# Mixing weights scaled and summed from an SBUF table, in place of fp32 kernel sums kept in DRAM: an adaptive mixing and FFN kernel on one Trainium2 core

## What is computed

```python
# cond: one 64x64 mixing matrix and a bias per sample
h = gelu(cond @ W0 + b0); h = gelu(h @ W1 + b1)
att = softmax(h @ W2 + b2)                         # [128 samples, K=8]
agg_w = einsum('bk,koi->boi', att, weight)         # [128, 64, 64]
agg_b = att @ bias_k
y = einsum('boi,bih->boh', agg_w, x) + agg_b[:, :, None]
# ffn on the rows of y (D = 1024)
base = einsum('bsd,od->bso', y, base_W)
logits = einsum('bsd,ed->bse', y, router_W)        # E = 8 experts, top 2
mid = einsum('bsd,edr->bser', y, lora_A) * gate    # R = 16
out = x + base + 2 * einsum('bser,erd->bsd', mid, lora_B)
```

## Time and profile before

| | |
|---|---|
| median of 3 runs | 992.72 us (991.69 to 1067.75) |
| the profiled execution | 992.38 us |
| its span | 990.6 us |
| mean granted TensorE clock | 0.989 |
| TensorE busy | 963.9 us, 97% |
| VectorE busy | 686.5 us, 69% |
| ScalarE busy | 208.7 us, 21% |
| GpSimd busy | 330.5 us, 33% |
| DMA | 115.00 MB, 64145 packets, 38392 of them under 512 B |

### The profile page before, as it was taken

How to read it: one execution, slowest core, us unless ns; L and a number is a source line. 1 busy time by engine, 2 the same in 40 slices (tenths; PEclk the granted TensorE clock), 3 DMA queues, 4 the chain that set the end, 5 groups by cost and what they waited for, 6 DMA issues and landing times.

```text
span 990.6 us, 17707 instructions
## 1 busy us (share of the span) xinstructions
PE 963.9 (97%) x5742; PEld 882.8 (89%) x5742; DVE 686.5 (69%) x1529; ACT 208.7 (21%) x422; POOL 330.5 (33%) x245
## 2 busy tenths in 40 slices
PE   6788999999999999999999999999999999999998
PEld 4577999999999999999999999999999999999996
DVE  2878676677676667767667776766776766677674
ACT  3432121122211211212121121211212112122120
POOL 4904333322333322333332233333223333223331
PEclk9889999999999999999999999999999999999999
DMA  8324333433423333332343333334333233433311
GB/s 281 100 122 136 103 106 115 135 108 111 128 93 114 120 132 111 112 113 93 114 135 117 116 122 101 105 114 135 109 111 133 90 115 117 134 109 112 120 48 54
DMA packets 64145, 115.00 MB, mean 116 GB/s; under 512 B 38392, under 2 KB 38520, under 8 KB 63480
## 3 DMA queue, kind: packets, MB, share of 16 engines
q1 hardware_dynamic: 63856, 114.76, 35.0%
q10 hardware_dynamic: 272, 0.03, 0.0%
HBM read 79.01 MB, written 35.68 MB: 116 GB/s over the span
## 4 chain that ended last, share of the span: by engine, by line
PE 91%; issue 4%; POOL 2%; DMA 1%; DVE 1%; SPq 0%; POOLq 0%; DVEq 0%
PE pc L504 17%; PE pa L515 13%; PE pb L515 13%; PE y_ps L476 11%; PE pb L518 9%; PE pa L518 9%; PE pd L504 9%; PE pc L536 4%; PE pd L536 4%; DMA c_raw<-in_base_t 1%; PE pd L526 1%; POOL w_raw L360 1%; POOL w_raw L348 1%; POOL lb_lo L395 0%; DVE out_sb L910 0%
## 5 line engine op out<-in xcount | busy, mean ns | idle before, releaser
L405 POOL TENSOR_TENSOR out_sb<-out_sb,u 128x512 f32<-128x512 f32 x96 | 136.4, 1451 | 209.1 <-DVE u L956 209.1
L476 PE MATMUL y_ps<-mix_w,x_sb 128*128 128x128 f32 x1024 | 199.5, 280 | 0.7 <-issue 0.7
L476 PEld LDWEIGHTS y_ps<-mix_w,x_sb 128*128 128x128 f32 x1024 | 171.9, 194 | 17.3 <-issue 3.9
L366 POOL TENSOR_TENSOR ya<-ya 128x512 f32<-128x512 f32 x32 | 42.6, 1331 | 420.7 <-DVE ya L850 420.7
L850 DVE TENSOR_TENSOR ya<-y_ps,bias_sb 128x512 f32<-128x512 f32 x128 | 87.7, 686 | 34.4 <-PE y_ps L476 31.3
L504 PE MATMUL pc<-w_hi,s_hi 128*128 128x512 f32 x256 | 106.8, 417 | 2.9 <-DVE out_sb L910 2.9
L515 PE MATMUL pa<-w_hi,a_hi 128*128 128x376 f32 x256 | 101.5, 397 | 6.2 <-DVE w_lo L802 6.2
L504 PE MATMUL pc<-w_hi,s_lo 128*128 128x512 f32 x256 | 101.2, 395 | 0.0
L504 PE MATMUL pc<-w_lo,s_hi 128*128 128x512 f32 x256 | 100.5, 393 | 0.0
L515 PE MATMUL pa<-w_lo,a_hi 128*128 128x376 f32 x256 | 86.3, 337 | 0.0
L515 PE MATMUL pa<-w_hi,a_lo 128*128 128x376 f32 x256 | 86.2, 337 | 0.0
(11 more groups left out here) (149 smaller groups left out, 2373.6 us busy)
## 6 DMA issues: line engine op xcount, KB each, us to landing
x_sb<-in_x SPq DMA_DIRECT2D x64, 512.0 KB, 3.4
out_sb<-in_x SPq DMA_DIRECT2D x64, 512.0 KB, 4.3
out<-out_sb SPq DMA_DIRECT2D x64, 512.0 KB, 2.8
bias_sb<-bias_rows SPq DMA_DIRECT2D x62, 64.0 KB, 5.2
agg_rows<-agg SPq DMA_DIRECT2D x1, 2048.0 KB, 9.1
mix_w<-agg_rows SPq DMA_DIRECT2D x120, 16.0 KB, 3.3
a_raw<-in_base_t SPq DMA_DIRECT2D x1, 1024.0 KB, 7.8
c_raw<-in_base_t SPq DMA_DIRECT2D x1, 1024.0 KB, 12.4
```

The source lines that it names most:

```text
L366: nc.gpsimd.tensor_tensor(y_block(0, 1), y_block(0, 1), y_block(0, 0), ALU.subtract).then_inc(s3_set, 1)
L405: nc.gpsimd.tensor_tensor(o, o, u2[:, :], ALU.add).then_inc(done, 1)
L476: mm = nc.tensor.matmul(y_ps[q % 2][:, j * P:(j + 1) * P], x_sb[m][:, c * P:(c + 1) * P], mix_w[m][:, :], start=True, stop=True)
```

## The change

The table mix_i (128 x 512: for each partition 64 outputs by 8 kernels, now laid out for both halves by the host and loaded in one DMA) stays in SBUF for the whole run. att_rows (128 x 512) holds for each partition its sample's eight attention values of all 64 tiles; it is made by one fp32 matmul from two small tables (parity, att_spread). For each tile n, m DVE multiplies the table with the tile's eight values (scale_mix) and sums over the kernels (sum_mix), and ACT copies the sum into the diagonal blocks (place_mix). The eight kernel sums, agg, agg_dram, mix_k and the DMAs of mix_w are gone. The scaled table of 128 x 512 lies over u2. b2 comes with params. The first loads stand in another order, and the warming transposes become fp32r matmuls of 512 columns. The core of the diff:

```diff
@@ sync
             sp.dma_start(mlp[:, :], params).then_inc(params_in, 16)
-            sp.dma_start(b2_sb[:, :], b2.partition_broadcast(P)).then_inc(b2_in, 16)
+            sp.dma_start(mix_i[:, :], mix_t).then_inc(mix_i_in, 16)
+            sp.dma_start(bk_sb[:, :], bias_k).then_inc(bk_in, 16)
             sp.dma_start(a_raw[:, :], base_t[0, :, :]).then_inc(a_in, 16)
-            for b in range(PAR):
-                sp.dma_start(mix_i[b * C:(b + 1) * C, :], mix_t).then_inc(mix_i_in, 16)
-            sp.dma_start(bk_sb[:, :], bias_k).then_inc(bk_in, 16)
-            for m in range(2):
-                sp.dma_start(x_sb[m][:, :], x_t[m, :, :]).then_inc(x_in[m], 16)
-            sp.dma_start(mix_k[:, :], mix_rows).then_inc(mix_k_in, 16)
+            sp.dma_start(x_sb[0][:, :], x_t[0, :, :]).then_inc(x_in[0], 16)
             sp.dma_start(w_raw[W_SIDE], side).then_inc(side_in, 16)
+            sp.dma_start(x_sb[1][:, :], x_t[1, :, :]).then_inc(x_in[1], 16)
...
                 next_x(n, m)
-                mixing_weights(2 * n + m, m, agg_dram)
                 mixing_bias(2 * n + m, m)
@@ tensor
-                    nc.tensor.transpose(pb[:, 0:P], ident[:, :], ident[:, :])
+                    nc.tensor.matmul(pb[:, 0:BANK], hot[:, 0:P], hot[:, :], start=True, stop=True)
...
-            pe.wait_ge(mix_k_in, 16)
-            mixing_kernels(0)
+            keep_warm(1)
             pe.wait_ge(bias_ready, 1)
...
             mm.then_inc(bias_bc_mm, 1)
+            keep_warm(2)
...
-                    if first(n):
-                        pe.wait_ge(mix_set[m], 2)
-                    else:
-                        pe.wait_ge(mix_w_in[m], MIX_W * n)
+                    pe.wait_ge(mix_set[m], PAR * n + PAR)
...
-                if q < 3:
-                    mixing_kernels(q + 1)
-            pe.wait_ge(agg_act, 2)
+                if q == 1:
+                    pe.wait_ge(spread_set, 1)
+                    nc.tensor.matmul(pb[:, BANK:], parity[:, :], att_spread[:, :], start=True,
+                                     stop=True).then_inc(att_rows_mm, 1)
@@ scalar
+            def place_mix(n, m):
+
+                act.wait_ge(summed_set, 2 * n + m + 1)
+                if first(n):
+                    act.wait_ge(zeros_set, 4)
+                else:
+                    act.wait_ge(mixed, 4 * n + m - 1)
                 for b in range(PAR):
...
@@ scalar, first_body
-                for n in range(4, NA):
-                    take_agg(n)
+                place_mix(1, 0)
                 for n in range(WP):
                     act.wait_ge(t1_made, n + 1)
                     take_hi(T1, n)
+                place_mix(1, 1)
                 act.wait_ge(lb_in, 16)
...
                 split_high(S3, 1, s3_set, 2)
+                place_mix(2, 0)
                 exponents(1)
                 split_high(A12, 1, y_ready, 8)
+                place_mix(2, 1)
@@ scalar, body
                     split_high(A12, p + 1, y_ready, 4 * p + 8)
+                mixes = not (isinstance(p, int) and p >= NP - 2)
+                if mixes:
+                    place_mix(p + 2, 0)
                 exponents(2 * p + 1)
+                if mixes:
+                    place_mix(p + 2, 1)
@@ vector
+            def scale_mix(n, m):
+
+                if first(n - 1 if isinstance(n, int) else n):
+                    dve.wait_ge(att_rows_set, 1)
+                dve.wait_ge(summed_set, 2 * n + m)
+                nc.vector.tensor_tensor(scaled[:, :].rearrange("p (c k) -> p c k", k=K),
+                                        mix_i[:, :].rearrange("p (c k) -> p c k", k=K),
+                                        att_rows[:, bass.ts(2 * n + m, K)].unsqueeze(1).broadcast_to(
+                                            [P, C, K]), ALU.mult).then_inc(scaled_set, 1)
+
+            def sum_mix(n, m):
+
+                dve.wait_ge(scaled_set, 2 * n + m + 1)
+                if not first(n):
+                    dve.wait_ge(mix_set[m], PAR * n)
+                nc.vector.tensor_reduce(summed[m][:, :], scaled[:, :].rearrange("p (c k) -> p c k", k=K), AX.X,
+                                        ALU.add).then_inc(summed_set, 1)
@@ vector, before the first body
             split_low(A12, 0)
+            scale_mix(1, 0)
+            sum_mix(1, 0)
             split_low(S3, 0)
@@ vector, first_body
                     take_lo(T3, n)
+                scale_mix(1, 1)
+                sum_mix(1, 1)
                 dve.wait_ge(t2_made, WP)
...
                 add_bias(1, 2)
+                dve.wait_ge(u2_in21, 1)
+                scale_mix(2, 0)
+                sum_mix(2, 0)
                 split_low(S3, 1)
...
                 split_low(A12, 1)
+                scale_mix(2, 1)
+                sum_mix(2, 1)
@@ vector, body
                 add_p5(p, k)
+                mixes = not (isinstance(p, int) and p >= NP - 2)
+                if mixes:
+                    dve.wait_ge(u2_in21, p + 1)
+                    scale_mix(p + 2, 0)
+                    sum_mix(p + 2, 0)
                 add_side_b(p)
                 add_up11_p74(p, k)
+                if mixes:
+                    scale_mix(p + 2, 1)
+                    sum_mix(p + 2, 1)
```

More of the change, by code:

```diff
@@ L3, with adaln_ffn_kernel @@
 from contextlib import ExitStack
-def adaln_ffn_kernel(nc, x, params, b2, mix_t, mix_rows, bias_k, base_t, side, lora_b, out):
+def adaln_ffn_kernel(nc, x, params, mix_t, bias_k, base_t, side, lora_b, out):
     f32, f32r = mybir.dt.float32, mybir.dt.float32r
@@ L112, in adaln_ffn_kernel @@
         _, warm = place("warm", 1)
+        _, mix_i = place("mix_i", C * K)
+        _, att_rows = place("att_rows", NT * K)
+        summed = [place(f"summed{m}", C)[1] for m in range(2)]
         assert top[0] <= 229344
@@ L132, in adaln_ffn_kernel @@
         b0_sb, b1_sb = (mlp[:, 3 * P + K + n:3 * P + K + n + 1] for n in range(2))
+        b2_sb = mlp[:, 3 * P + K + 2:3 * P + 2 * K + 2]
         h1, h2 = (over(f"h{n}", P, mlp_at + (3 + n) * P * 4 + 256) for n in range(2))
-        mix_i = over("mix_i", C * K, p1_at)
-        scaled = [over(f"scaled{m}", C * K, at) for m, at in enumerate((u2_at, s1_at))]
-        summed = [over(f"summed{m}", C, side_b_at + m * C * 4) for m in range(2)]
+        scaled = over("scaled", C * K, u2_at)
         pick_row = over("pick_row", 2 * PAR * P, ya_at)
         pick_half = over("pick_half", 2 * PAR * C, ya_at + 2 * PAR * P * 4)
+        hot = over("hot", BANK, ya_at + 2 * PAR * (P + C) * 4, f32r)
+        parity = over("parity", P, s2_at)
+        parity2 = over("parity2", PAR, s2_at + P * 4)
+        own_tile = over("own_tile", NT, s2_at + 2 * P * 4)
+        att_spread = over("att_spread", NT * K, s1_at)
         att_t = over("att_t", B, mid_at, parts=K)
@@ L141, in adaln_ffn_kernel @@
         bias_rows = over("bias_rows_sb", C, mid_at + 768)
-        att, b2_sb, att_n, att_nm, att_sum = (over(f"att{n}", c, mid_at + 1024 + n * 32) for n, c in enumerate(
-            (K, K, K, 1, 1)))
+        att, att_n, att_nm, att_sum = (over(f"att{n}", c, mid_at + 1024 + n * 32) for n, c in enumerate(
+            (K, K, 1, 1)))
         pa = ctx.enter_context(nc.psum_tensor("pa", [P, 2 * BANK], f32))
@@ L197, in adaln_ffn_kernel @@
         ROUTE = 12
-        NA = C * C // BANK
         def first(p):
@@ L256, in mixing_bias @@
                              bias_dram.rearrange("s (t r) -> t s r", t=NT)[t, :, :].partition_broadcast(P)
[L257 to L265, removed]
-                    else:
-                        src = agg_dram[r, :].rearrange("(i s c) -> i s c", i=C, s=2)
-                    sp.dma_start(dst[:, :, b, :], src).then_inc(mix_w_in[m], 16)
+                             ).then_inc(bias_in[m], 16)
             def next_x(n, m):
@@ L421, in keep_warm @@
                 for _ in range(times):
-                    nc.tensor.transpose(pb[:, 0:P], ident[:, :], ident[:, :])
[L424 to L433, removed]
+                    nc.tensor.matmul(pb[:, 0:BANK], hot[:, 0:P], hot[:, :], start=True, stop=True)
+            pe.wait_ge(hot_set, 1)
             pe.wait_ge(consts_set, 1)
-            keep_warm(3)
+            keep_warm(2)
             pe.wait_ge(params_in, 16)
@@ L692, in _ @@
                           bias_rows[:, :].rearrange("b (s c) -> b s c", s=2)).then_inc(bias_out, 16)
-            place_mix(0)
+            place_mix(0, 0)
             act.wait_ge(bias_bc_mm, 1)
@@ L698, in _ @@
                                ).then_inc(bias_set, 1)
-            take_agg(0)
-            place_mix(1)
-            take_agg(1)
+            place_mix(0, 1)
             act.wait_ge(side_in, 16)
```

78 lines of the change are left out of this document (35 added, 43 removed).

## The result

The changed kernel takes 1029.38 us (median of 4 runs, 1028.64 to 1030.52) against 993.0 (median of 4): a ratio of 1.0372, with a 95% interval of 1.0352 to 1.0392. One of the four runs of the kernel before took 1067.75 us, 7.6% above the other three, and is left out of the ratio. The forecast was 1036.4, in a range of 1015 to 1051, slower.

What follows compares the result with a forecast made beforehand. PE was taken to bound the kernel, busy 97% of the span and throughout the steady pairs. 992.4 + 29 x 1.6 for the pairs + 2.1 for the first body - 4.5 for the start = 1036.4 us, range 1015 to 1051.

Steps and rivals of the forecast that it cites:

- The pair: Steady loop: mid_lo comes late, so PE idles 1.6 us before up(0) in each of 29 pairs.
- the first place: After add_p5, before add_side_b: the first scaling waits for POOL, leaving the DVE queue 0.56 us late.
- the DRAM trip: Two copies of mixing weights from DRAM per tile, already hidden since PE never waits; removing them is worth 0.
- The address from a register: Scalings in the loop read att_rows at a register address; cost taken as 0, with 0.4 as the other end.
- The first pair: First body: same pieces, tighter, with POOL beside both scalings; loss of 2.1 us, bounds 1 and 3.
- rival C: PE idle time before up(0) lowers its clock to half speed in each pair: 1089 us, chance 0.04.
- The start: Before the steady pairs: earlier mixing brings B21's end forward; gain of 4.5 us, bounds 2 and 8.
- the parity product: New fp32 matmul with 512 columns in the start, taken to cost PE 2.0 us.
- the removed sums: Four of eight kernel sums gone before the first mixing, counted with the 3.53 us mix_k wait as 11.5 us.
- A: Delay stays hidden because DVE's idle 8.7 us a pair swallow the new 2.8: 987.9 us, chance 0.12.
- B: Queue order delays but no turns at the DVE/POOL port: 1.0 us a pair, 1019 us, chance 0.22.
- D: Much better start, all five waits and the eight sums' share gone, delay hidden: 970 us, chance 0.02.

Runs made afterwards that it cites:

- e1: Changed kernel with only ACT's copies of the second tile's sum moved behind mid_hi and keep_p1 of the next body: 1005.13 us, ratio 1.0125.
- e3: Changed kernel with only the second tile's scaling and sum moved into DVE's gap ahead of the even tile's routing: 986.87 us, ratio 0.9938.
- e4: Changed kernel with only the first tile's scaling and sum moved into DVE's gap ahead of the even tile's routing: 1021.61 us, ratio 1.0292.
- e2: Changed kernel with both tiles' scalings and sums moved into DVE's gap ahead of the even tile's routing: 985.88 us, ratio 0.9933.
- b1: Kernel before the change, with four of its kernel sums moved behind the first pair's mixing and ACT's copies moved too: 986.47 us, ratio 0.9943.
- e5: e2 with the first scaling of pair 1 reading the attention rows from PSUM, before they are copied: 984.86 us, ratio 0.9928.
- s1: e2 with the small warming transposes of the kernel before in place of the large warming matmuls: 985.83 us, ratio 0.9936.

## Why the prediction was right

**The pair.** The mechanism was right at each step: the scaling held by POOL at the first place, no gain from the DRAM trip, ACT standing in front of place_mix(p + 2, 1) with the two splits and mid_hi queued behind, mid_lo late, PE idle in front of up(0) once per pair. e1, e3 and e4 show each part by itself. e2 shows that the work itself is free. The size was 1.35 in place of 1.6. The term that was mis-sized is the first place: the 0.56 us by which the DVE queue was to be late there were 0.28. From u2 to POOL's third sum's end it took 315.91 - 306.91 = 9.00 before and, with L363 at 292.51 lasting 1.28, 293.79 - 284.51 = 9.28 after. I had let the scaling end 0.65 behind POOL's first sum; it ended 0.54 behind it (291.38 against 290.84). And I had let POOL's next sum start anew there and cost its full 1.30; it had started at 290.91, lasted 1.63 and ended at 292.54, 1.16 behind the scaling. So some 0.14 us of it ran beside the scaling. The address from a register cost nothing that shows: the second scaling takes 0.68, and the profile has 64 ns on DVE's sequencer for it.

**The first pair.** Taken at 2.1; it cost 5.0 - 2.8 = 2.2 up to up(0) of body 1, a wait of 2.86 less the 0.65 that is gone. But the wait there was 2.86 us long, and what I had kept as rival C happened here, once. The windows of the changed kernel behind it, and those of e1, where the wait at the same place was 2.05 (up(0) at 84.73):

```profile
87.00:88.00 1.00, 1.00 (x4) 0.81 (x3) 0.83 (x2) 0.33 (x1) 0.00 (x0) 0.50 0.00 0
...
91.00:92.00 1.00, 1.00 (x9) 1.00 (x8) 0.00 (x0) 0.00 (x0) 0.00 (x0) 1.00 0.95 205
```

```profile
85.00:86.00 1.00, 1.00 (x6) 0.77 (x5) 1.00 (x3) 0.00 (x0) 0.00 (x0) 1.00 0.99 401
...
87.00:88.00 1.00, 1.00 (x9) 1.00 (x8) 1.00 (x3) 0.00 (x0) 0.00 (x0) 1.00 0.00 0
```

After 2.86 us of idleness the granted clock was 0.50, the level of 1.2 GHz, in the three windows from 87 to 90, and 0.80 in the next; after 2.05 it stayed at 1.00, as it did after the 2.14 of e4 and the 1.1 of the later pairs. This term of 31.95 - 29.13 - 1.36 = 1.5 us was missing from my sum.

**The start.** Taken at 4.5, 5.0 at 77.55. Right with wrong parts: the mixing ended at 20.5 and not at 23.6, as its passes became twice as fast within it (sixteen took 2.05) and the parity product took 1.0 in place of 2.0. But of these 11.3 us DVE and POOL passed on only 7 to the B21 product (39.01, forecast 41.5) and 5.5 to the T2 product. I had put the gain down to the removed sums; b1 shows that it was their place, on PE or on ACT. I had not seen the 10.50 us for which DVE waited for ACT.

**The sum.** 992.4 + 29 x 1.35 + 2.2 + 1.5 - 5.0 = 1030.2 with the measured terms, where the profiled execution took 1030.03. Rivals A, B and D are out by the period, B by e5 and by the 1.55 us of the first scaling as well; C holds in one pair of thirty.

## What to carry to other kernels

Idle time of an engine, as a share or per iteration, says that new work fits, not where. For each place read what is queued behind it on that engine and on the engine that consumes it: the same 2.8 us on DVE cost 39 us in the second half of the body and nothing in the gap ahead of a wait for PE. When an in-order engine has to wait for a new result, put its copy behind everything that the bound engine needs next; and before replacing work in a start, try to move it behind the work that others are waiting for.

## What the runs showed of the hardware

An instruction of POOL that started 0.47 us before the end of a DVE instruction with two SBUF operands lasted 0.33 longer (1.63 in place of 1.30). Multiplying 128x512 fp32 with one operand in PSUM took 0.68 beside POOL; with both in SBUF it took 1.55 and 1.75 in the rows shown (0.68 beside an idle POOL). All 64 sums over 128x512, with one operand in SBUF, took 0.69 in the changed kernel, beside POOL or not; a copy inside SBUF was held by POOL all the same (0.78, at its shortest 0.17).

fp32 mixing passes of the same shape took 0.25 us each for 14 us in the kernel before (17.78 to 31.82), with 8-partition kernel sums between them and the granted clock given as 1.00, and 0.13 in the changed kernel from 18.41 on. The fp32r products behind them were slow too: L515, 376 columns, took 0.52 at 32.70 and 0.34 at 33.64. So the granted clock of the first 33 us doesn't show what the passes show. s1 rules out the warmers as the cause, b1 is at 0.24 with no kernel sum between, and what decides stays open.
